# Projection products shifted to the even steps of an attention stage, and a reordered start of its setup

## The reference

```
mod = silu(condition) @ Wada + bada                 # six vectors of 512 per sequence
sh_a, sc_a, gt_a, sh_m, sc_m, gt_m = split(mod, 6)
xm = layernorm(x, g1, be1) * (1 + sc_a) + sh_a
x = x + gt_a * attention(xm, Wqkv, Wproj, bproj)    # causal, 16 heads of 32
xm = layernorm(x, g2, be2) * (1 + sc_m) + sh_m
x = x + gt_m * (gelu(xm @ W1 + b1) @ W2 + b2)
```

## Time and profile before

| | |
|---|---|
| median of 3 runs | 3634.16 us (3627.92 to 3637.36) |
| the profiled execution | 3628.45 us, its span 3626.7 us |
| PE busy | 3427.0 us, 94% |
| DVE busy | 1793.7 us, 49% |
| ACT busy | 1202.2 us, 33% |
| POOL busy | 1017.7 us, 28% |

### The profile page before, as it was taken

How to read it: one execution, slowest core, us unless ns; L and a number is a source line. 1 busy time by engine, 2 the same in 40 slices (tenths; PEclk the granted TensorE clock), 3 DMA queues, 4 the chain that set the end, 5 groups by cost and what they waited for, 6 DMA issues and landing times.

```text
span 3626.7 us, 59043 instructions
## 1 busy us (share of the span) xinstructions
PE 3427.0 (94%) x19052; PEld 2415.8 (67%) x19052; DVE 1793.7 (49%) x2386; ACT 1202.2 (33%) x2578; POOL 1017.7 (28%) x1265
## 2 busy tenths in 40 slices
PE   6889999999999999998884999999999999999999
PEld 3545555555555555553333998999899988998898
DVE  3355655655655656655534444444444444444442
ACT  2134554554554554544551111111111111211111
POOL 1222222222222222222224323333333333333332
PEclk8889999999999999999997999999999999999999
DMA  5445555555555555554434122212221222122220
GB/s 199 135 128 162 150 162 154 156 153 159 152 162 152 155 155 157 151 154 135 132 94 132 50 63 63 69 50 69 55 69 49 69 55 69 54 65 55 69 58 12
DMA packets 227209, 392.77 MB, mean 108 GB/s; under 512 B 30160, under 2 KB 96720, under 8 KB 227080
## 3 DMA queue, kind: packets, MB, share of 16 engines
q1 hardware_dynamic: 213648, 369.42, 35.4%
q10 hardware_dynamic: 13440, 22.03, 1.7%
HBM read 271.71 MB, written 119.11 MB: 108 GB/s over the span
## 4 chain that ended last, share of the span: by engine, by line
PE 88%; DVE 5%; ACT 3%; issue 2%; DMA 1%; POOL 0%; ACTq 0%; SPq 0%; DVEq 0%; POOLq 0%
PE psH L720 20%; PE psY L733 20%; PE psA L633 14%; PE psA L578 9%; PE psT L610 9%; PE psP L699 5%; PE psA L574 5%; PE psS L592 4%; DVE mx L1027 3%; ACT e L802 2%; DVE psS L1025 1%; PE psP L709 1%; ACT xm_full L780 1%; PE psT L538 1%; PE psA L557 1%
## 5 line engine op out<-in xcount | busy, mean ns | idle before, releaser
L802 ACT ACTIVATE e<-psT 128x512 f32<-128x512 f32 (+3 forms) x1536 | 680.3, 492 | 811.7 <-PE psT L610 786.1
L1251 POOL TENSOR_TENSOR h_l<-h_full,h_h 128x256 fp32r<-128x256 f32 x512 | 488.4, 954 | 1121.3 <-DVE h_h L1177 1121.3
L1027 DVE TENSOR_REDUCE mx<-psS 128x4 f32<-128x2048 f32 (+3 forms) x384 | 675.4, 1759 | 217.6 <-PE psS L592 208.8
L902 ACT ACTIVATE h_full<-psH,b1c 128x256 f32<-128x256 f32 x512 | 243.9, 476 | 1332.3 <-PE psH L720 1332.3
L1177 DVE CAST h_h<-h_full 128x256 fp32r<-128x256 f32 x512 | 150.1, 293 | 899.6 <-ACT h_full L902 899.6
L720 PE MATMUL psH<-a_h,w1p_h 128*128 128x256 f32 x2048 | 577.8, 282 | 7.5 <-DVE a_l L1172 7.5
L633 PE MATMUL psA<-e,vst 128*33 128x512 f32 (+3 forms) x3072 | 580.8, 499 | 0.6 <-POOL e L1277 0.2
L720 PE MATMUL psH<-a_h,w1p_l 128*128 128x256 f32 x2048 | 580.3, 283 | 0.0
L720 PE MATMUL psH<-a_l,w1p_h 128*128 128x256 f32 x2048 | 579.9, 283 | 0.0
L610 PE MATMUL psT<-qst,kst 97*128 97x512 f32 (+3 forms) x1536 | 517.6, 396 | 46.8 <-ACT e L802 42.7
L1277 POOL TENSOR_SCALAR_AFFINE_SELECT e<-e 128x256 f32<-128x256 f32 x512 | 228.9, 449 | 1070.9 <-ACT e L802 1070.4
(11 more groups left out here) (97 smaller groups left out, 3945.0 us busy)
## 6 DMA issues: line engine op xcount, KB each, us to landing
qk_split<-qk_hl SPq DMA_DIRECT2D x128, 512.0 KB, 3.2
kst<-qk_split SPq DMA_DIRECT2D x128, 256.0 KB, 4.0
qst<-qk_split SPq DMA_DIRECT2D x128, 256.0 KB, 4.3
values<-vaug ACTq DMA_DIRECT2D x64, 264.0 KB, 2.1
vst<-values SPq DMA_DIRECT2D x32, 528.0 KB, 4.0
attended<-o_sb SPq DMA_DIRECT2D x256, 66.0 KB
xin<-in_x_dram SPq DMA_DIRECT2D x64, 256.0 KB, 4.5
kmx<-qk_split SPq DMA_DIRECT2D x32, 512.0 KB, 4.3
```

Of the source, the lines that this page charges most:

```text
L802: act.activation(e[:, s % ERING, hd, 0:w], psT[:, hd, 0:w], ACT.Exp, scale=SCALE)\
L902: act.activation(h_full[:, m % 4, :], psH[:, m % 4, 0:RA], ACT.Gelu, bias=b1c[:, m:m + 1])\
L1027: dve.tensor_reduce(mx[:, part, :, qt], psS[:, :, 0:w], AX_X, ALU.max).then_inc(sem("max_reduced"), 1)
L1251: return pool.tensor_tensor(dst, full, high.bitcast(F32), ALU.subtract)
```

## The change

The shares of an item's products become a table by step, `A_SHARES`. An item of three steps that begins in an even step has 6, 0, 6 products; the next one, which begins in an odd step, 2, 8, 2; and the one of four steps 5, 1, 5, 1. Even steps so carry 5, 6 or 8 products, odd ones 0, 1 or 2. Which item runs over which steps, and where its first part stands, stays.

In the setup VectorE does the layer norm of block 0 first, then the modulation of vector 0, low part 0, the modulation of vector 1, the coefficients and low part 2. GpSimd takes low parts 1 and 3, between its power and its half of `xm_l`. TensorE waits for the low parts behind the turns of block 0. The modulation of the last four vectors moves to block 1, between its turns and its items, on TensorE; on VectorE behind the split of block 1's `xm`. Its store on SyncE moves behind all stores of block 1.

```diff
-A_LENGTHS = (3, 3, 4) * 4
+A_SHARES = ((6, 0, 6), (2, 8, 2), (5, 1, 5, 1)) * 4
@@ def item_at(s):
-    for n, length in enumerate(A_LENGTHS):
-        if s < length:
-            return n, s, length
-        s -= length
+    for n, shares in enumerate(A_SHARES):
+        if s < len(shares):
+            return n, sum(shares[:s]), sum(shares[:s + 1])
+        s -= len(shares)
@@ def item_ended(s):
-    return at[0] if at and at[1] == at[2] - 1 else None
+    return at[0] if at and at[2] == A_MM and at[1] < A_MM else None
@@ SyncE, setup
                     a_store(ia, n)
-                if ia == 0:
-                    store_modulation(2, 6)
+            store_modulation(2, 6)
@@ TensorE, setup
-            pe.wait_ge(sem("wqkv_lo"), KT)
             for ia in range(AHEAD):
                 for k in range(A_TURNS):
                     a_turn(ia, k, True)
+                if ia == 0:
+                    pe.wait_ge(sem("wqkv_lo"), KT // 2)
+                    pe.wait_ge(sem("wqkv_lo_pool"), KT // 2)
+                if ia == 1:
+                    modulation(2, 6)
                 for n in range(A_ITEMS):
-                    a_item(ia, n, 0, 1, True)
+                    a_item(ia, n, 0, A_MM, True)
...
-                if ia == 0:
-                    modulation(2, 6)
@@ VectorE, setup
-            modulation(0, 2)
-            dve.wait_ge(sem("small_loaded"), 5 * 16)
-            coefficients(0, 0, 1)
-            for k in range(KT):
-                wqkv_low(k)
...
             layer_norm(0)
+            modulation(0, 1)
+            wqkv_low(0)
+            modulation(1, 2)
+            dve.wait_ge(sem("small_loaded"), 5 * 16)
+            coefficients(0, 0, 1)
+            wqkv_low(2)
             for ia in range(AHEAD):
                 a_split(ia)
                 a_split_low(ia)
+                if ia == 1:
+                    modulation(2, 6)
+                    coefficients(1, 3, 4)
...
-                if ia == 0:
-                    modulation(2, 6)
-                    coefficients(1, 3, 4)
@@ GpSimd, setup
             a_rstd(0)
+            for k in (1, 3):
+                pool.wait_ge(sem("wqkv_hi"), k + 1)
+                low(wqkv_l[:, k, :], wqkv[:, k, :], wqkv_h[:, k, :]).then_inc(sem("wqkv_lo_pool"), 1)
```

More of the change, by code:

```diff
@@ L558, in a_turn, with a_item @@
                 mm.then_inc(sem("a_formed"), 1)
-            def a_item(ia, n, part, parts, alone):
+            def a_item(ia, n, first, end, alone):
                 bank = n % 2 if alone else 1
-                if part == 0:
+                if first == 0:
                     if n == 0:
@@ L568, in a_item @@
                     wait(pe, sem("a_copied"), ia * A_N + A_TURNS + n - int(alone))
-                for q in range(A_MM * part // parts, A_MM * (part + 1) // parts):
+                for q in range(first, end):
                     k = q // 3
@@ L578, in a_item @@
                         mm = pe.matmul(psA[:, bank, :], w[:, k, m * P:(m + 1) * P], a[:, k, :], **ends)
-                if part == parts - 1:
+                if end == A_MM and first < A_MM:
                     mm.then_inc(sem("a_formed"), 1)
```

## The result

The changed kernel takes 3579.26 us (median of 4, 3575.83 to 3582.35) against 3634.7 us before: ratio 0.985, 95% interval 0.9832 to 0.9868. The forecast was 3589, its range 3565 to 3614. The profiled execution took 3576.45 us, 52.0 less than the one of before.

A forecast was written before the change was run, and what follows sets the result against it. Bodies with projection work were taken as mostly bound by TensorE, the setup by a chain through the engines. 3628.45 - 20.4 (setup) - 24.7 (bodies) = 3583.4 us profiled; with the median 5.7 above, 3589, range 3565 to 3614.

The forecast's parts named there:

- Setup, 20.4 forecast: Whole setup: 12.7 us from block 0's start, 6.3 from the modulation, 1.4 from the clock; range 17 to 21.5.
- GpSimd's slowness: Block 0's start: GpSimd's low parts put the first product at 34.0, between 33.1 and 34.6 at its slow duration.
- The sentence on the Trainium skill: Block 0: VectorE and GpSimd block each other for whole instructions; by this rule first product about 34.4, gain 12.3 us.
- The modulation's 6.3 us: Block 1: modulation of the last four vectors covers scaling and splits behind the turns, 18.0 us in place of 24.3.
- The clock term: Block 1's first 48 products start with a busy TensorE at the higher clock; gain 1.4 us, bounds 0 and 1.5.
- The moved store: SyncE's modulation store ahead of the loads for the first maxima; taken as 0, with 1 us lost as the bound.
- Bodies, 1.9 us forecast: Thirteen bodies: 1.3 us from pairs of scores plus 0.55 in steps 0 to 3; 24.7 us in all, bounds 9 to 30.
- the steps named: Waiting second scores in steps 7, 17, 29 (0.27 us each), 9 and 37 (0.23 each), plus steps 0 to 3 (0.55).
- the measure of an undisturbed pair: Two scores of 384 columns that nothing holds were taken as 0.61 us, against 0.84 when waiting.
- Setup only: Rival: waits in the bodies move instead of going, so only the setup gains; 3614 us, chance 0.15.
- More than counted: Rival: bodies also close nearly all of TensorE's 2.8 us not busy, 3.5 us a body; 3569 us, chance 0.14.
- The slower rival: ScalarE's copies after items 6, 0, 6 delay the next even step's scores, 3.2 us a body; 3644 us, chance 0.05.

The follow-up runs named there:

- e3: Changed kernel, but only items of four steps have the new shares (5,1,5,1), the others 4,4,4; 107.35 us a body, 3583.98 us in a single run.
- e1: Changed kernel with the old shares (4,4,4 and 3,3,3,3), so the new setup alone; 3614.34 us, ratio 0.9939.
- e4: Changed kernel, but only items of three steps have the new shares, those of four steps 3,3,3,3; 108.16 us a body, 3602.09 us in a single run.
- e2: Kernel before the change with the new shares alone, old setup kept; 3597.95 us, ratio 0.9895.
- e6: Changed kernel with shares the other way round (3,6,3 / 5,2,5 / 2,4,2,4); 113.68 us a body, 3674.47 us in a single run.
- e9: Changed kernel plus unread identity turns on TensorE behind even steps' scores in the last three bodies; 3564.56 us, ratio 0.9811.
- e7: Changed kernel with two bodies in each turn of the loop on every engine, body 1 written out; 3579.21 us.
- e10: Changed kernel with bodies 1 to 11 written out, no loop on any engine; 3575.17 us, ratio 0.9839.
- e8: Changed kernel with low part 3 on VectorE in place of GpSimd; 3566.88 us in one run, first product at 32.23 us.

## Why the prediction came out as it did

**The direction and the mechanisms were right, and the sizes of both halves were off, in opposite ways.** The gain forecast was 45 us, measured 52 in the profiles and 55 in the medians.

**Setup, 20.4 forecast, 17.9 measured.** Block 0's first product was put at 34.0 and came at 35.39. The chain was the forecast one, the scaling behind the coefficients. Two terms differ. The first, 1.0 us, is no more than one setup scatters: the scaling began at 25.87, not 24.85, because the coefficients were ready at 25.83, not 24.47. TensorE's 16 products of the modulation took 9.99 us, where they had 8.79 before. PEld's rows show why, for the trace after:

```profile
18.22 0.14 PEld L537 LDWEIGHTS psT<-wada,sT 128*8 128x8 f32 x1 [0.72 <-issue]
19.07 0.12 PEld L537 LDWEIGHTS psT<-wada,sT 128*8 128x8 f32 x1 [0.72 <-issue]
19.53 0.09 PEld L537 LDWEIGHTS psT<-wada,sT 128*8 128x8 f32 x1 [0.34 <-issue]
```

The products come every 0.85 us up to 19.07 and every 0.43 from there on, the two levels of the clock; the trace's record of the clock has its rise at 19.11 us, and at 16.54 in the trace of before. In the fourteen profiles the rise lies between 15.88 and 19.22 us and the coefficients are ready between 23.86 and 26.07, on the whole later where it is later; what sets the rise was not tried. With the changed kernel's setup the first product so spreads from 33.71 to 35.58 us.

The second term, 0.4 us, is the path from the scaling to the first product: 9.52 us, where the prediction had 8.26 and 0.9 for GpSimd's slowness. GpSimd wasn't slow by itself. The working let its half of xm_l start at 29.6, it started at 31.61, since VectorE's low part was held by GpSimd's second and the rounding came behind it. The sentence on the Trainium skill ("SBUF — State Buffer", "Who interferes with whom") gave 34.4 with the coefficients at 24.47. In e3, where they were ready at 24.40, the first product came at 34.24, and in e1 (24.26) at 34.37, nearer to that than to the 34.0 of the sum. The changed kernel and e3 show its rule in both orders.

The modulation's 6.3 us became 5.5: the turns of block 1 now follow block 0's items at once, and the second must wait for ScalarE's copy of the last item out of its bank, which the modulation had hidden. The modulation starts 73.21 - 70.29 = 2.9 us behind the last product, not 2.1. The clock term was right: 11.11 us for 48 products in place of 12.49. The moved store cost nothing to be seen: from block 2's first product to the first score it takes 66.9 us, 66.8 before.

**Bodies, 1.9 us forecast, 2.74 measured, and 1.66 of it in the steps named.** Steps 6 to 9, 16 to 19, 26 to 29 and 36 to 39 gained 0.66, 0.29, 0.30 and 0.41 us (means of bodies 2 to 11), where the prediction had 0.50, 0.27, 0.27 and 0.23. Steps 0 to 5 gained 0.48, forecast 0.55, and in the way forecast: the maxima of step 3 no longer wait for VectorE, since the second score of step 2 waits for ScalarE, until 4.89 us after the start of body 6 (forecast 4.8). The addition behind it was off: 4.8 + 0.1 + 1.4 + 0.3 is 6.6 us, not 6.5. On the mean of the ten bodies the maxima start 6.55 us after the start and 6.96 before, a gain of 0.41. The other 0.59 us lie in the other six items of three steps, 0.05 to 0.12 us each, for which the prediction had nothing.

**The step that failed is the measure of an undisturbed pair.** The prediction took 0.61 us for two scores of 384 columns that wait for nothing, from 906.81 in body 6. That pair waits too. PEld's rows of before show it, for steps 13 (the pair from 906.81) and 21:

```profile
906.98 0.19 PEld L610 LDWEIGHTS psT<-qst,kst 97*128 97x128 f32 x1 [0.21 <-ACT e L802]
...
924.73 0.19 PEld L610 LDWEIGHTS psT<-qst,kst 97*128 97x128 f32 x1 [0.21 <-ACT e L802]
```

Undisturbed it is 0.51, as after the change. So steps 9 and 37 had 0.33 to gain, not 0.23, and an even step with four products was too short as well. With 0.23 us taken off for each product that moved, steps 13, 21, 25 and 33, of 384 columns behind four products, are 0.11 to 0.13 us shorter after the change, and steps 5 and 31, of 512 columns, 0.07 and 0.08. The rule "three products are too few" should have been "fewer than five". e4 (items of three steps alone: 0.9 us) and e3 (107.35 with 4,4,4 left in) show this part apart.

Body 12, with no turns behind its items, gained 4.1 us and body 0 3.5. How these come about was not taken apart.

**The rivals.** "Setup only" falls with e2, whose bodies gain 2.3 us by themselves, 2.5 without the one with the lower clock. "More than counted" had the right side, and the result lies between it and the forecast, but not for its reason: it let the 2.8 us go in which TensorE isn't busy at all, and those stayed; what went were covered waits, more of them than the 1.6 us counted. The slower rival, copies in front of the exponentials, didn't happen; no score at the start of an even step of body 6 waits for one. e6 shows another way to lose, even steps that are too short: 4.6 us a body more than in e1.

## What to carry to other kernels

Where two engines pass work to and fro step by step, compare each step's own work with the partner's chain, not the sums: the 33 us of products in a body cost 15 or 13 us by where they stood, and the threshold (five products) mattered, not the place of the rest. Take the measure of "waits for nothing" from the smallest of many such pairs, and look at the weight loads too, which show idle time that overlapping matmuls cover. And look at stretches that the change doesn't touch: here the last three bodies scattered by 11 us from run to run, more than several of the effects under study, and filling them gained 12 us.

## What the runs showed of the hardware

- TensorE's clock in the last three bodies: PE is busy for 239 to 242 of 281 to 284 us there, and the mean granted clock is 0.94 to 0.95; it is at the lower of its two levels (1.2 GHz of 2.4) for 27.3 to 34.1 us in all. With turns of the identity between (e9), it is there for 3.4 us, and the stretch is 11 us shorter.
- The clock's first rise in the setup comes at 15.88 to 19.22 us in the fourteen profiles. While it is low, one product of the modulation takes 0.85 us, then 0.43; the first product of block 0 spreads by 1.9 us from profile to profile with one setup.
- The jump back of this loop costs at different places by the loop's length. With one body a turn, ScalarE's exponential of step 1 comes 1.5 us late and TensorE's jump shows nothing; with two (e7), ScalarE has nothing at that place and TensorE's first score waits 2.10 us with no releaser shown; with no loop (e10) both are gone. Why TensorE's jump is free in the one and not in the other was not tried.
- VectorE and GpSimd hold each other for whole instructions: 1.75 us became 4.65 on VectorE, 1.22 became 2.86, and GpSimd's 3.43 became 4.59. With GpSimd's second low part the path from the first scaling to the first product takes 9.48 to 9.83 us, without it (e8) 8.28.
